# Attention scores with the two heads of a pair in two 64-row halves of TensorE, and their maximum added by four 32-row products

## The reference

```python
xn = group_norm(x, gamma, beta)                      # 32 groups
q, k, v = split(w_qkv @ xn + b_qkv, 3)               # 8 heads of 64 channels, 1024 positions
weight = softmax((q * scale).T @ (k * scale), -1)    # 1024 x 1024 for each of 64 batch-heads
a = weight @ v
out = x + w_proj @ a + b_proj
```

## Time and profile before

| | us |
|---|---|
| median of 3 runs (lowest, highest) | 2893.01 (2890.81, 2893.12) |
| the profiled execution | 2894.75 |
| its span, first to last instruction | 2893.2 |
| mean granted clock of TensorE, share of 2.4 GHz | 0.986 |

### The profile page before, as it was taken

How to read it: one execution, slowest core, us unless ns; L and a number is a source line. 1 busy time by engine, 2 the same in 40 slices (tenths; PEclk the granted TensorE clock), 3 DMA queues, 4 the chain that set the end, 5 groups by cost and what they waited for, 6 DMA issues and landing times.

```text
span 2893.2 us, 36061 instructions
## 1 busy us (share of the span) xinstructions
PE 2768.7 (96%) x11860; PEld 1816.3 (63%) x11860; DVE 1854.5 (64%) x2429; ACT 1243.0 (43%) x1535; POOL 1142.5 (39%) x531
## 2 busy tenths in 40 slices
PE   8999999998999999999999989999999899999998
PEld 6888878886655655575457545655665465557555
DVE  5554445555677557847774777478657856774776
ACT  3232222223456245525553464356345525553443
POOL 3310000001455355616661654355345625661662
PEclk9999999998999999999999999999999999999999
DMA  5331011121001110121012011201110121012001
GB/s 182 127 107 58 29 43 43 58 91 69 15 23 52 60 44 26 48 89 37 19 36 100 23 37 44 74 22 37 52 67 22 51 76 44 18 40 102 15 15 59
DMA packets 59315, 155.94 MB, mean 54 GB/s; under 512 B 8704, under 2 KB 8704, under 8 KB 59136
## 3 DMA queue, kind: packets, MB, share of 16 engines
q1 hardware_dynamic: 55552, 141.07, 13.9%
q0 software_dynamic: 3584, 12.58, 1.3%
HBM read 111.69 MB, written 41.94 MB: 53 GB/s over the span
## 4 chain that ended last, share of the span: by engine, by line
PE 81%; DVE 10%; issue 5%; ACT 3%; POOL 0%; ACTq 0%; DVEq 0%; POOLq 0%
PE psum L1103 16%; PE psum L1324 13%; PE psum L1285 13%; PE psum L1309 11%; PE psum L1291 8%; DVE small L938 6%; PE psum L1122 6%; PE psum L1146 3%; PE psum L1174 3%; PE psum L1338 2%; PE psum L1217 2%; PE psum L1114 1%; ACT a_all L671 1%; PE psum L1220 1%; PE psum L1358 1%
## 5 line engine op out<-in xcount | busy, mean ns | idle before, releaser
L506 POOL TENSOR_TENSOR a_all<-a_all 128x1024 f32<-128x1024 f32 x441 | 1066.6, 2418 | 1098.5 <-ACT a_all L671 786.3
L938 DVE TENSOR_REDUCE small<-psum 128x1 f32<-128x512 f32 x1024 | 687.3, 688 | 280.0 <-PE psum L1291 275.0
L671 ACT ACTIVATE a_all<-psum 128x1024 f32<-128x1024 f32 x512 | 512.4, 1024 | 439.0 <-PE psum L1309 425.3
L1309 PE MATMUL psum<-r_all 128*128 128x512 f32 x2048 | 599.4, 398 | 21.0 <-ACT a_all L671 18.4
L1291 PE MATMUL psum<-r_all 128*128 128x512 f32 x1024 | 440.3, 436 | 60.3 <-DVE small L938 46.0
L1324 PE MATMUL psum<-a_all 128*64 128x512 f32 x2048 | 496.8, 606 | 0.0
L1103 PE MATMUL psum<-r_all 128*128 128x512 f32 x1920 | 463.4, 402 | 4.9 <-DVE r_all L1004 4.9
L1309 PEld LDWEIGHTS psum<-r_all 128*128 128x128 f32 x2048 | 383.8, 189 | 118.7 <-ACT a_all L671 33.4
L1103 PEld LDWEIGHTS psum<-r_all 128*128 128x128 f32 x1920 | 368.7, 194 | 100.2 <-DVE a_all L963 11.4
L1291 PEld LDWEIGHTS psum<-r_all 128*128 128x128 f32 x1024 | 190.0, 188 | 329.7 <-DVE small L938 166.0
L1285 PE MATMUL psum<-r_all 128*128 128x512 f32 x1536 | 386.7, 401 | 10.7 <-DVE r_all L1023 5.5
(11 more groups left out here) (117 smaller groups left out, 2030.3 us busy)
## 6 DMA issues: line engine op xcount, KB each, us to landing
r_all<-w_dram SPq DMA_DIRECT2D x48, 1024.0 KB, 5.1
a_all<-y_dram SPq DMA_DIRECT2D x9, 2048.0 KB, 7.9
a_all<-x SPq DMA_DIRECT2D x16, 1024.0 KB, 6.3
y_dram<-a_all SPq DMA_DIRECT2D x16, 1024.0 KB, 4.2
out<-a_all SPq DMA_DIRECT2D x32, 512.0 KB, 3.0
a_all<-y_dram SPq DMA_DIRECT2D x56, 256.0 KB, 2.7
w_dram<-r_all POOLq DMA_DIRECT2D x16, 512.0 KB, 3.0
a_all<-w POOLq DMA_DIRECT2D x16, 256.0 KB, 3.0
```

The source lines that it names most:

```text
L506: pool.tensor_tensor(p_sum[:, h], probs[:, 0, h] if i == 1 else p_sum[:, h], probs[:, i % 2, h], ALU.add).then_inc(sum_step, 1)
L671: act.activation(probs[:, i % 2, h], psum[h][:, :, :].rearrange("p a n -> p (a n)"), ACT.Exp, scale=SCALE).then_inc(probs_ready, 1)
L938: dve.reduce_max(max2[:, h, tile, half:half + 1], ps, AX_X).then_inc(work_free, 1)
L1309: last = pe.matmul(psum[h][:, half], k, q[:, half * HALF:(half + 1) * HALF], start=first, stop=not first)
```

## The change

The two heads are taken side by side in the rows of the array. `q_hl` and `k_hl` hold HI and LO of both heads, each head in its own 64 partitions. A product of 64 rows for head 0 (rows 0 to 63) is followed at once by that for head 1 (rows 64 to 127), into another bank. psum0 now holds the first 512 queries of both heads, psum1 the second. For each key tile `scores` issues four 32-row products of `ones_r` with `mx` (one for each head and half, in rows 32 r to 32 r + 31, into four banks), and then for each half three pairs of 64-row products. `max_tile` issues a pair of 64-row products into both banks of psum3, which one DVE reduction over 128x2x512 reads: 16 a pair of heads in place of 32. `probs` has three slots in place of two. `sums` is one call of four products into psum2, where there were two of two into psum3. The copies by ACT (L611, L617) and the half-height ACT and DVE instructions of `qk_hi` and `qk_lo` become one of full height. In the first layer `xt` shares memory with `gs`.

The order changes as well. The transpose of the maxima follows the first q/k tile of the next pair rather than the end of the pair; all four q/k tiles come before the first scores; two `max_tile` stand in each key tile. `max_tile` waits until all tiles of psum3 are free.

```diff
-        R_SIZE, A_SIZE = 152 * 256, 50 * 256
+        R_SIZE, A_SIZE = 136 * 256, 60 * 256
...
-        xt = r0.take(XT_SLOTS, 2, C)
         gs = us = r0.take(2, CT, C)
+        xt = gs.rearrange("p a j c -> p (a j) c").rearrange("p (s a) c -> p s a c", a=2)
...
+                        for half in range(1 if last_pair else NH):
+                            cols = slice(half * HALF, (half + 1) * HALF)
+                            if i == 1 and half == 0:
+                                pool.wait_ge(sums_full, ONE + pairs)
+                            pool.wait_ge(probs_ready, ONE + pairs * 2 * NT + 2 * i + half + 1)
...
+                            pool.tensor_tensor(p_sum[:, :, cols], probs[:, 0, :, cols] if i == 1 else p_sum[:, :, cols],
+                                               probs[:, i % SLOTS, :, cols], ALU.add).then_inc(sum_step, 1)
...
+                act.activation((q_hl, k_hl)[of_k][:, par, HI, cols], ps, ACT.Identity,
+                               bias=bqkv_c[:, of_k * CT + pair:of_k * CT + pair + 1]).then_inc(qk_hi_done, 1)
...
+            def max_tile(m):
+                n = work.next_pair()
+                half, tile = m // NT, m % NT
                 dve.wait_ge(work_full, n)
-                dve.reduce_max(max2[:, h, tile, half:half + 1], ps, AX_X).then_inc(work_free, 1)
+                dve.reduce_max(max2[:, :, tile, half], psum[3][:, :, :], AX_X).then_inc(work_free, 2)
...
+                dve.tensor_tensor(mx.rearrange("p (j t) -> p j t", j=HT), ps[:, 0:P].unsqueeze(1).to_broadcast([P, HT, P]),
+                                  mask[:, :, :], ALU.mult).then_inc(work_free, 1)
...
                     next_qk(0)
+                    max_rows(pairs)
                     if p:
-                        invert_sums(b, p - 1, 0)
+                        invert_sums(pairs - 1, 0)
                     next_qk(1)
                     if p:
+                        invert_sums(pairs - 1, 1)
                     next_qk(2)
                     next_qk(3)
+                    def between(m):
+                        if p:
+                            if m in (0, 1):
+                                normalise(pairs - 1, m)
+                            if m in (6, 8):
+                                hid_lo(b, p - 1, (m - 6) // 2)
...
+                        if p == 2 and not last:
+                            for u in range(NH * CT):
+                                if LO_AT[u] == m:
+                                    norm_lo(b + 1, u)
...
+            def max_tile(par, m):
+                half, tile = m // NT, m % NT
+                n = work.next_pair()
+                pe.wait_ge(work_free, n - 2)
+                for h in range(2):
+                    rows_ = slice(h * D, (h + 1) * D)
+                    last = pe.matmul(psum[3][:, h], q_hl[rows_, par, HI, tile * P:(tile + 1) * P],
+                                     k_hl[rows_, par, HI, half * HALF:(half + 1) * HALF], start=True, stop=True)
+                last.then_inc(work_full, 2)
...
+            def scores(pairs, par, i):
+                keys = slice(i * P, (i + 1) * P)
+                for half in range(NH):
+                    pe.wait_ge(probs_ready, ONE + pairs * 2 * NT + (2 * (i - 1) + half + 1 if i else 0))
+                    for h in range(2):
+                        r = slice((h * NH + half) * ROWS, (h * NH + half + 1) * ROWS)
+                        pe.matmul(psum[half][:, h], ones_r[r], mx[r], start=True, stop=False)
+                for half in range(NH):
+                    cols = slice(half * HALF, (half + 1) * HALF)
+                    for t, (k, q) in enumerate(((HI, HI), (LO, HI), (HI, LO))):
+                        for h in range(2):
+                            rows_ = slice(h * D, (h + 1) * D)
+                            last = pe.matmul(psum[half][:, h], k_hl[rows_, par, k, keys], q_hl[rows_, par, q, cols],
+                                             start=False, stop=(t == 2))
+                    last.then_inc(scores_full, 1)
...
+            def sums(pairs, last=False):
+                pe.wait_ge(o_ready, ONE + pairs + 1)
...
+                    pe.wait_ge(sum_step, ONE + (pairs + 1) * ADDS)
...
                     next_qk(0)
+                    turned = max_turn(pairs)
+                    if p:
+                        sums(pairs - 1)
+                    for i in range(1, QK):
+                        next_qk(i)
+                    next_max(0)
+                    pe.wait_ge(work_free, turned)
+                    scores(pairs, par, 0)
+                    next_max(1)
+                    for i in range(1, NT):
+                        scores(pairs, par, i)
+                        next_max(2 * i)
+                        weigh(b, p, i - 1)
+                        if i < NT - 1:
+                            next_max(2 * i + 1)
+                    weigh(b, p, NT - 1)
+                    next_max(MAXES - 1)
```

More of the change, by code:

```diff
@@ L130, in build @@
         o32 = a1.take(N)
[L131 removed]
+        recip = a1.take(NH, HALF)
         SMALL = 732
@@ L696, in batch1 @@
                     if more:
-                        work.next()
-                        q_b_hi(par)
+                        for _ in range(MAXES):
+                            work.next_pair()
                     act.wait_ge(hid_lo_done, ONE + pairs * NH)
@@ new lines, in batch1 @@
+                pairs = b * PAIRS + PAIRS - 1
+                if last:
+                    for h in range(NH):
+                        invert_sums(pairs, h)
+                        normalise(pairs, h)
+                        hid_lo(b, PAIRS - 1, h)
+                else:
+                    for i in range(NT):
+                        v_tile(b + 1, i)
+                        if i in (1, 2):
+                            invert_sums(pairs, i - 1)
+                        if i in (3, 4):
+                            normalise(pairs, i - 3)
+                        if i in (5, 6):
+                            hid_lo(b, PAIRS - 1, i - 5)
@@ L1300, in v_tile @@
                                       for j in range(CT) for w, m in THREE]).then_inc(work_full, 1)
-            def scores(pairs, par, i, between):
-                for h in range(2):
-                    pe.wait_ge(probs_ready, ONE + pairs * 2 * NT + 2 * max(i - 1, 0) + (h + 1 if i else 0))
-                    keys = slice(i * P, (i + 1) * P)
-                    for first, (k, q) in ((True, (k_a[:, par, h, keys], q_a[:, par, h])), (False, (k_b[:, par, h, keys], q_b[:, h]))):
-                        for half in range(NH):
-                            last = pe.matmul(psum[h][:, half], k, q[:, half * HALF:(half + 1) * HALF], start=first, stop=not first)
-                            if not first and half == NH - 1:
-                                last.then_inc(scores_full, 1)
-                            between(4 * h + 2 * (not first) + half)
@@ L1424, in turn, with next_max @@
-                    def turn(place):
-                        if more and place == 9:
-                            max_turn(pairs + 1)
-                    weigh(b, p, NT - 1, turn)
-                for i in range(NT):
-                    if not last:
-                        v_tile(i)
-                    if i in (2, 4):
-                        sums(b * PAIRS + PAIRS - 1, i // 2 - 1, bank(i // 2 - 1), end_sums_full, last)
+                    def next_max(m):
+                        if more:
+                            if m < 2:
+                                pe.wait_ge(qk_hi_done, (pairs + 1) * QK + 3 + m)
+                            max_tile(1 - par, m)
```

368 lines of the change are left out of this document (136 added, 232 removed).

## The result

| kernel | median us (lowest to highest, runs) | ratio, 95% interval | span of the profiled execution | mean granted clock |
|---|---|---|---|---|
| before | 2892.33 (2890.81 to 2893.12, 4) | 1 | 2893.2 | 0.986 |
| after | 2938.07 (2932.70 to 2940.25, 4) | 1.0156 [1.0138, 1.0174] | 2935.0 | 0.971 |

The change makes the kernel 1.6% slower. I had said 2857 us and 64% for faster. The time lies inside the range of 2815 to 2955, the direction is wrong. In the profiled execution 36 us were to be gained and 42 were lost: 78 us have to be found.

What follows compares the result with a forecast made beforehand. PE, 96% busy, was taken as the bound: its list plus its waits. Section changes summed to -4.6 us a batch, -36 in all, taking the profiled 2894.75 to 2858.8 and the median to 2857 us; range 2815 to 2955.

Steps and rivals of the forecast that it cites:

- The tile: PE's work per key tile: nine slots, `weigh` and three row-grouping changes, 4.53 us against 5.69 before.
- serial loads: Rival: weights load one after another in the row groups, +0.52 us a tile, 2982 us in all; 10%.
- products one after another: Rival: products in different rows don't run side by side, 20 slots for 9 a tile, 3490 us; 5%.
- changes at 0.40: Rival: each grouping change between 32 and 64 rows costs 0.40 us, +0.4 a tile, 2952 us; 10%.
- They cost nothing: Rival: grouping changes between 32 and 64 rows are free, -0.4 us a tile, 2817 us; 15%.
- Does DVE follow?: One-buffer psum3: a pair of maxima is free after 1.82 us, PE returns after 2.2 or 2.35, so hidden.
- T to U: From the end of a pair's work to the start of `sums`: 3.2 us by PE, 3.6 where POOL holds it.
- Values, projection, pair 0: Batch section from values through pair 0: 97.8 us against 99.08, -1.3, with four q/k tiles, wait and maximum at 13.6.
- DVE against POOL: DVE's SBUF operations wait for POOL's adds: +1.3 us in pairs 1 to 3, 9.3 for ten in pair 2.
- The clock: PE's granted clock was read as 1.00, the upper level of 2.4 GHz.
- The start of a pair: PE waits 1.8 us before the first maximum and 1.3 for ACT before tile 1; scores begin 12.45 after `sums` starts.
- POOL becomes a second bound: POOL's 14 adds take 34.4 us a pair and hold `sums` by 0.4 in pairs 1.

Runs made afterwards that it cites:

- e4_rows64: Kernel after with the maximum's term as two pairs of 64-row products with zero weights, replacing four 32-row products: 2878.42 us, 0.9955 of before.
- e3_spread: Kernel after with DVE's SBUF operations in pair 2 spread so that no maximum has two behind it: 2917.24 us, 1.0082 of before.
- e8: Kernel after with six useless products filling PE's wait before the first maximum of each pair: 2920.73 us, 1.0103 of before.
- e10: e1_early with six useless products added in the wait before the first maximum of each pair: 2887.77 us, 0.9995 of before.
- e6_all: Kernel after with last maxima earlier, pair 0's transpose first, DVE operations spread, 64-row maximum terms, each half issued when free: 2775.62 us, 0.9595 of before.
- e1_early: Kernel after with the last maxima of each pair of heads placed before the last weighted values: 2898.20 us, 1.0018 of before.

## Why the prediction was wrong, step by step

- **The tile**: right. 4.53 predicted, 4.54 measured. The products run side by side in rows, and the loads of four row groups do too. That strikes out three rivals: serial loads (0.19 for four, not 0.11 each), products one after another, and changes at 0.40. "They cost nothing" falls as well: e4_rows64 gives 0.20 for each change. What the prediction lacked was the next question, whether the 32-row products are worth their two changes.
- **"Does DVE follow?"**: the failing step. The working of 1.82 us until a pair of maxima is free is right, and so is the answer inside the pair. It was not asked at the two ends, where other work takes psum3's banks: the last maxima are followed at once by a q/k or a value tile. The order of after's PE stream shows this adjacency, and 1.82 less the maxima's 0.43 gives the 1.40 that was found. Term: T to U, 3.2 predicted, 4.5 measured, 31 times, **43.4 us**.
- **"Values, projection, pair 0"**: the four q/k tiles were taken as an unbroken row. The wait of the second for L895, eight times 1.46, is **11.6 us**. In the other pairs `sums` stands in between and hides it, which the prediction put to use without seeing what pair 0 lacks.
- **"DVE against POOL"**: right mechanism, too small where the clock falls. Ten operations at 0.93 each were taken from before's pair 2. There each stood alone behind a maximum with two buffers ahead; now two stand in a row behind maximum 6, and PE has no buffer left. 65.6 against 62.0 is 3.6, less the 1.40 already counted 2.2, over seven batches **15 us**. The trace says more: the two pairs 2 that have only 6.8 us at the lower clock take 62.98 and 63.59, what was predicted with the 1.40 (63.4), although the 3.17 is in them too. All of the 15 lies in the other five, so the row of two costs this much only together with the longer fall of the clock. Which of the two starts the other is not shown; spreading the row (e3_spread) took away both. In pair 0 and in pair 3 with the values 0.3 and 0.7 remain beside the known waits, some **8 us** in all. 43.4 + 11.6 + 15 + 8 = 78, the whole gap.
- **The clock**: I read 1.00 in the earlier trace rows and took it as given. It fell in the new gaps. Its part, 13 to 25 us by e8 and e10, lies inside the 15 and the 8 and can't be added to them. In pair 3 with the values five windows with 3.4 us at the lower level take 103.5 to 103.7, and the two at 1.00 take 102.6 and 101.6, close to the 101.1 and 1.40 of the known terms: so the 0.7 there is the clock as well.
- **The start of a pair**: right. 1.56 for 1.8 before the first maximum, 32 times 49.1 us in all. The wait for ACT before tile 1 was to be 1.3 and is 0.34 and 0.41; over the kernel 30.0 us against 32 x 1.3 = 42.
- **"POOL becomes a second bound"**: not in the kernel after, where its adds end at 1688.98 and `sums` starts at 1691.34, since PE was later than I had it. POOL's timeline of the 14 adds:

```profile
1654.10 34.88 POOL L497 TENSOR_TENSOR a_all<-a_all 128x1024 f32<-128x1024 f32 x14 [19.88 <-ACT a_all L651]
```

34.88 against 34.4. In e6_all the same mechanism holds `sums` ten times, eight of them at the start of a pair 1, where the prediction had looked for it.
- **The rival on the other side** was a mechanism that is not there (0.40 a change). The slower time came from a case with no chance of its own: the buffers of psum3 held at the ends of a pair. With it the sum would have been 2857 + 43 = 2900, and with the 11.6 of pair 0 2912. That 2938 lies inside the range is luck: the upper end was put at 2955 for the changes at 0.40.
- **Slips in the sums**, none of which decides anything: 1789.07 to 1836.4 is 47.3, not 47.2; 4.2 and 3.2 us a pair over 32 pairs are 134 and 102, not 125 and 95, unless POOL's slack, which only the last rival names, is taken off there too.

## What to carry to other kernels

When two buffers are merged so that one instruction reads both, look at every consumer of these buffers: not only the loop in which the reader keeps up, but the first and last turn of it, where other work takes the same banks. Write down, from the new order, each pair of neighbours that use them, and the time between the two. And where packing changes the row grouping, count the changes, not only the slots: packing by two with zero weights beat packing by four. Issue what is ready in each half before waiting for the other one.

## What the runs showed of the hardware

- Four 32-row products of 512 columns in four row groups run side by side, 0.43 us from the first of them to the next block. Twelve 64-row products in pairs take 1.37, six slots of 0.229, where no change follows. The Trainium skill ("TensorE: Matmul & The Clock Gate", Part 3: Packing small matmuls) gives 3.07 times the speed for four products of 32 rows. Measured against four slots of 0.229 the four with both changes took 0.64 (a slot and 0.41), 1.4 times: the concurrency is there, but a group of only four products doesn't earn its changes.
- In the kernel after the granted clock falls to 1.2 GHz after the wait of 1.56 us at the start of five pairs 3 and four other pairs, in a pair 2 by the end of the wait of 3.17, and there in five once more behind a wait of 0.9 to 1.4 for ACT: 112.2 us in the second layer against 23.8 before. With the 1.56 filled (e8_fill) it stays at 1.00 in seven windows of pair 3 and values. It did not fall after each of the 32 waits of 1.56: the windows of 53.80 and 55.95 us above hold one each, at 1.00. The same pair 1 took 54.82 us at 1.00 and 56.64 at 0.94 (e1_early).
- A DVE operation on SBUF of 0.68 us took 2.27 behind a POOL add, and the one right behind it 2.85.
